# Two windowed-attention layers: the tile order of all engines, the cosine product's source and the layout of the keys

## The reference, cut to what matters

```python
h = shift_token(x)                     # second half of the channels from the token before
q, k, v = split(h @ wqkv, 3)           # 512 wide each
q = l2norm(q) * qs; k = l2norm(k) * ksc
q = q * cos * scale + rotate_half(q) * sin * scale
k = k * cos / scale + rotate_half(k) * sin / scale
# local attention: 64 queries see the 64 keys of their own window and the 64 of the window before
sim = (q * 8) @ k.T; sim = where((i < j) | (i > j + 64) | (j == -1), -max, sim)
o = softmax(sim) @ v
x = x + o @ wo
x = x + gated_gelu_mlp(layer_norm(shift_token(x)))
```

## Time and profile before

| | us |
|---|---|
| median of 3 runs | 1483.24 (1483.23 to 1484.29) |
| the profiled execution | 1488.5, of which the span from first to last instruction is 1486.8 |
| window stage of layer 0, from its first instruction to its last residual | 633.9 to 955.6 |
| window stage of layer 1 | about 1047 to 1368.8 |
| busy in the span: PE, DVE, ACT, POOL | 1283.7, 1194.9, 933.0, 743.3 |

### The profile page before, as it was taken

How to read it: one execution, slowest core, us unless ns; L and a number is a source line. 1 busy time by engine, 2 the same in 40 slices (tenths; PEclk the granted TensorE clock), 3 DMA queues, 4 the chain that set the end, 5 groups by cost and what they waited for, 6 DMA issues and landing times. The chain is left out here.

```text
span 1486.8 us, 30399 instructions
## 1 busy us (share of the span) xinstructions
PE 1283.7 (86%) x10501; PEld 712.6 (48%) x10501; DVE 1194.9 (80%) x3044; ACT 933.0 (63%) x2597; POOL 743.3 (50%) x742
## 2 busy tenths in 40 slices
PE   4579999999999997359999999699689999996992
PEld 2323333343333333326666666555356666665551
DVE  5577888888888860669999999666599999996667
ACT  4415777777677674647888888332378888884220
POOL 2001212221221221469999999210599999993102
PEclk9757999999999997679999999899899999999896
DMA  5412111112111001001211111000002111110001
GB/s 116 134 62 68 36 56 48 37 36 61 43 37 49 24 6 67 31 22 30 50 30 30 30 30 30 8 1 1 21 23 51 33 32 31 30 30 9 1 1 57
DMA packets 35056, 55.46 MB, mean 37 GB/s; under 512 B 6978, under 2 KB 22732, under 8 KB 32588
## 3 DMA queue, kind: packets, MB, share of 16 engines
q1 hardware_dynamic: 34328, 53.37, 13.5%
q10 hardware_dynamic: 576, 0.15, 0.0%
HBM read 26.77 MB, written 8.39 MB: 24 GB/s over the span
## 5 line engine op out<-in xcount | busy, mean ns | idle before, releaser
L512 ACT ACTIVATE a_prob<-a_psE 128x512 f32<-128x512 f32 (+3 forms) x768 | 318.6, 500 | 142.7 <-PE a_psE L440 140.3
L428 PE MATMUL a_psM<-a_ks,a_qs 72*128 72x512 bf16 (+3 forms) x768 | 252.3, 347 | 17.4 <-PEq L76 15.2
L595 DVE CUSTOM_DVE_ANT_0 a_psM<-a_psM,mask_q 128x384 f32<-128x384 f32 (+3 forms) x512 | 242.4, 507 | 30.7 <-PE a_psM L428 30.1
L440 PE MATMUL a_psE<-a_qs,a_ks 84*128 84x512 bf16 (+3 forms) x768 | 250.7, 339 | 16.5 <-ACT a_prob L512 8.3
L1082 POOL TENSOR_TENSOR w_t<-w_raw,w_sin 128x256 f32<-128x256 f32 x256 | 240.1, 966 | 46.9 <-ACT w_raw L1008 46.9
L547 POOL TENSOR_SCALAR_AFFINE_SELECT a_prob<-a_prob 128x512 f32<-128x512 f32 x128 | 81.1, 635 | 335.7 <-ACT a_prob L512 311.1
L597 DVE TENSOR_REDUCE a_nm<-a_psM 128x1 f32<-128x512 f32 x256 | 175.8, 687 | 47.3 <-PE a_psM L428 47.3
L1031 ACT ACTIVATE w_prob<-w_psS,w_bias 128x128 f32<-128x128 f32 x512 | 180.9, 366 | 48.8 <-DVE w_bias L1160 43.2
L1092 POOL TENSOR_TENSOR w_rn<-w_ssm,mhalf 128x16 f32<-128x16 f32 x64 | 189.4, 2959 | 0.0
L440 PEld LDWEIGHTS a_psE<-a_qs,a_ks 84*128 84x128 bf16 x768 | 75.0, 98 | 181.3 <-ACT a_prob L512 97.1
L1087 POOL TENSOR_TENSOR w_rot<-w_t 128x1024 f32<-128x1024 f32 x64 | 152.9, 2389 | 8.8 <-issue 0.4
(11 more groups left out here) (139 smaller groups left out, 2529.9 us busy)
## 6 DMA issues: line engine op xcount, KB each, us to landing
w_vb<-w_v SPq DMA_DIRECT2D x128, 128.0 KB, 2.3
a_qs<-q_parts SPq DMA_DIRECT2D x16, 576.0 KB
a_ks<-k_parts SPq DMA_DIRECT2D x16, 576.0 KB
q_parts<-p_parts SPq DMA_DIRECT2D x24, 128.0 KB
k_parts<-p_parts SPq DMA_DIRECT2D x24, 128.0 KB
out_x<-l_y SPq DMA_DIRECT2D x8, 256.0 KB, 2.3
a_qs<-a_nmT SPq DMA_DIRECT2D x32, 48.0 KB
w_wqkv<-in_wqkv SPq DMA_DIRECT2D x2, 768.0 KB, 7.2
```

The lines of the kernel that those rows point to most:

```text
L428: pe.matmul(out, qs[0:ROWS, g, j, i * P:(i + 1) * P], ks[0:ROWS, g, j, 512 * kc:512 * kc + n], start=True, stop=True).then_inc(m_ready, 1)
L440: pe.matmul(psE[:, r % NRING, 0:w], ks[0:KROWS, g, j, kt * P:(kt + 1) * P], qs[0:KROWS, g, j, q0:q0 + w], start=True, stop=True).then_inc( ...
L512: act.activation(prob[G % NPROB][:, j, 0:w], psE[:, r % NRING, 0:w], ACT.Exp, scale=SCALE0).then_inc(e_read, 1)
L595: dve.tensor_tensor_reduce(scores, scores, sb["mask_q"][:, 512 - n:512], -1.0, -3.0 * NEG, ALU.add, ALU.min, low).then_inc(m_read, 1)
```

## The change

It touches `window` alone, and the mask constant of that stage.

- **The lists.** Each slot now projects q and k of tile s+2 and v of tile s+1, turns and scores tile s-1, and weights tile s-2; tile s-3 is put out first. Slots run from -2 to NT+2. `turn_p` is cut: its first half stands ahead of `scores`, its second behind. On DVE `normalise`, `divide` and `residual` stand first.
- **POOL** does norms(t) and then rotate(t), of the same tile.
- **The cosines** are multiplied straight from psQK in PSUM instead of from raw, and t1 has two buffers. `project_qk` therefore also waits for t1_done, and `copy_raw` no longer does.
- **The keys** of a batch lie in one row, kT[P, 2, 4, 64 + 1024], and each tile is copied to its place behind the one before. The copy L1153 and its semaphore are gone; both windows' scores read 128 keys in a row from there. The order of keys changes with it, so v's copy and the mask change halves.

```diff
-        t1, t2 = tile("w_t1", [P, 2 * INNER]), tile("w_t2", [P, 2 * INNER])
+        t1, t2 = tile("w_t1", [P, 2, 2 * INNER]), tile("w_t2", [P, 2 * INNER])
-        qT, kT = tile("w_qT", [P, 2, 4, P]), tile("w_kT", [P, 2, 4, KEYS])
+        qT, kT = tile("w_qT", [P, 2, 4, P]), tile("w_kT", [P, 2, 4, WIN + S])
...
-            for s in range(NT + 4):
-                slot(s, s % 4, False)
+            for s in range(-2, NT + 3):
+                slot(s)
...
                     at_least(pe, raw_done, base, t, 0)
+                    at_least(pe, t1_done, base, t, 0)
...
+                half, first = t // TB % 2, t % TB * P
                 for c in range(4):
                     cols = slice(c * P, (c + 1) * P)
...
+                    for u in range(2):
+                        for w in range(2):
+                            rows = slice(DH * w, DH * w + DH)
+                            i = pe.matmul(psS[WIN * u:WIN * u + WIN, w, cols], qT[rows, p, c, WIN * u:WIN * u + WIN],
+                                          kT[rows, half, c, first + WIN * u:first + WIN * u + P], start=False, stop=True, skip_group_check=True)
...
-                for used in (t1_done, t2_done):
-                    at_least(act, used, base, t, -1)
+                at_least(act, t2_done, base, t, -1)
...
-                pool.tensor_tensor(rot[:, r % 2, :], t1[:, :], t2[:, :], ALU.add).then_inc(rot_done, 1)
+                pool.tensor_tensor(rot[:, r % 2, :], t1[:, r % 2, :], t2[:, :], ALU.add).then_inc(rot_done, 1)
...
-            pipelined(pool, NT, 4, [(1, norms), (0, rotate)])
+            for t in range(NT):
+                norms(t, t % 4)
+                rotate(t, t % 4)
...
-                at_least(dve, rot_done, base, t, 0)
-                dve.tensor_tensor(t1[:, :].rearrange("p (w h d) -> p w h d", w=2, d=DH), raw[:, r % 2, :].rearrange("p (w h d) -> p w h d", w=2, d=DH),
+                at_least(dve, rot_done, base, t, -1)
+                dve.tensor_tensor(t1[:, r % 2, :].rearrange("p (w h d) -> p w h d", w=2, d=DH), psQK[:, :, :].rearrange("p w (h d) -> p w h d", d=DH),
                                   cos[:, t % TB, :, :].unsqueeze(2).broadcast_to((P, 2, HEADS, DH)), ALU.mult).then_inc(t1_done, 1)
...
-                at_least(dve, prev_copied, base, t, 0)
-                dve.tensor_copy(kT[:, p, :, 0:P], psT[:, 1, :].rearrange("p (c n) -> p c n", c=4)).then_inc(kT_copied, 1)
-
-                halves(dve, s_done, t, -2)
-                dve.tensor_copy(kT[:, p, :, P:KEYS], kT[:, 1 - p, :, WIN:P]).then_inc(prev_copied, 1)
+                dve.tensor_copy(kT[:, t // TB % 2, :, WIN + t % TB * P:WIN + t % TB * P + P],
+                                psT[:, 1, :].rearrange("p (c n) -> p c n", c=4)).then_inc(kT_copied, 1)
```

More of the change, by code:

```diff
@@ L917, in scores @@
                               sb["mask_w"][:, t % TB, :].unsqueeze(1).broadcast_to((P, 4, P)), start=True, stop=False, skip_group_check=True)
+                half, first = t // TB % 2, t % TB * P
                 for c in range(4):
                     cols = slice(c * P, (c + 1) * P)
[L920 to L926, removed]
-                        i = pe.matmul(psS[WIN:P, w, cols], qT[rows, p, c, WIN:P], kT[rows, p, c, 0:P], start=False, stop=True, skip_group_check=True)
+                    for u in range(2):
[3 more added lines that the diff above has]
+                                          kT[rows, half, c, first + WIN * u:first + WIN * u + P], start=False, stop=True, skip_group_check=True)
                 i.then_inc(s_done, 2)
@@ L1177, in residual, with slot @@
                 dve.tensor_tensor(sb["xf"][:, t, :], sb["xf"][:, t, :], psO[:, 0:P], ALU.add).then_inc(xf_done, 1)
-            def slot(s, r, whole):
+            def slot(s):
                 def runs(t):
-                    return whole or 0 <= t < NT
-                r2, r3 = (r - 2) % 4, (r - 3) % 4
+                    return 0 <= t < NT
+                if runs(s - 1):
+                    normalise(s - 1, (s - 1) % 4)
                 if runs(s - 2):
-                    copy_kT(s - 2, r2)
+                    divide(s - 2, (s - 2) % 4)
                 if runs(s - 3):
-                    divide(s - 3, r3)
-                if runs(s - 4):
-                    residual(s - 4, r)
-                if runs(s):
-                    cosines(s, r)
-                if runs(s - 2):
-                    maxima(s - 2, r2, 0)
-                if runs(s + 2):
-                    carry(s + 2, (r + 2) % 4)
-                if runs(s - 3):
-                    copy_pT(s - 3, r3)
-                if runs(s - 1):
-                    normalise(s - 1, (r - 1) % 4)
-                if runs(s - 2):
-                    maxima(s - 2, r2, 1)
-                if runs(s):
-                    sums(s, r)
+                    residual(s - 3, (s - 3) % 4)
+                if runs(s - 1):
+                    copy_kT(s - 1, (s - 1) % 4)
+                if runs(s + 1):
+                    cosines(s + 1, (s + 1) % 4)
+                if runs(s - 1):
+                    maxima(s - 1, (s - 1) % 4, 0)
+                if runs(s - 2):
+                    copy_pT(s - 2, (s - 2) % 4)
+                if runs(s - 1):
+                    maxima(s - 1, (s - 1) % 4, 1)
+                if runs(s + 1):
+                    sums(s + 1, (s + 1) % 4)
+                if runs(s + 3):
+                    carry(s + 3, (s + 3) % 4)
             carry(0, 0)
-            carry(1, 1)
             slots(dve, slot)
@@ L1506, in constants @@
     c["c_sel"] = sel
[L1509 to L1510 removed]
+    ok = (i % WIN <= j) & (j <= i % WIN + WIN)
     mask = np.broadcast_to(ok[:, None, :], (P, TB, P)).copy()
[L1512 removed]
+    mask[:WIN, 0, :WIN] = False
     c["c_mask_w"] = np.where(mask, 0.0, NEG).astype(bf)
```

96 lines of the change are left out of this document (42 added, 54 removed).

## The result

The changed kernel is slower by 1.4%: 1506.19 us, median of 4 runs (1505.26 to 1507.16), where the kernel before, run beside it, took 1483.76 us (1483.23 to 1485.10, 4 runs). The ratio is 1.0141, with a 95% interval of 1.0129 to 1.0154. The forecast was 1473.0, with a range of 1453 to 1482. The profiled execution took 1506.04, its span 1504.3, at a mean granted clock of 0.931 (0.926 before).

The account below looks back on a forecast made before the run. The prediction took a closed chain of PE with DVE, 9.12 us a tile, as the bound; with fill and drain it won 5.1 us a layer, so 1478.3 profiled, less 5.26 to the median: 1473.0 us, range 1453 to 1482.

Parts of the forecast that it names:

- PE's chain: Closed chain of PE with DVE, once a tile in mid stage: claimed to set the period at 9.12 us (9.06 to 9.18).
- Now four transposes stand there, about 0.45: On PE, between the transposes of q and k and the scores: about 0.45 us of work standing there.
- The last term: End of PE's chain: DVE's copy of the keys, 0.69 us, and 0.06 to PE, where the next mask begins.
- the last slots: Drain of a layer, last three slots: 8.5, 8.25 and 11.2 us, set at 28.0 together.
- The fill: Start of a layer: bounded by POOL, with the scores of tile 2 starting at 676.0 us.
- POOL's turn without the lock: POOL's work a tile once the sine products are not held up: 8.19 us, 0.97 less.
- The signs named ahead: Signs in the profile: period 9.06 to 9.18 us, two PE waits a tile, POOL idle about 1 us a tile.
- A loop of DVE: Rival: DVE's loop, with its wait for the scores, sets the period at about 8.8 us, 1456 in all; chance 0.14.
- The lock was avoided: Rival denied here: cosines from PSUM still block POOL's sine products, period 9.2 to 9.25 us, 1478 in all; chance 0.10.
- The product from PSUM: Rival: the cosines' product from PSUM is slow; at twice 1.22 us it adds 0.5 a tile, 1500; chance 0.05.
- The power didn't hold up DVE: Rival denied here: normalise and divide wait 2.95 us for POOL's power, 1592 us in all; chance 0.01.
- PE's clock: Rival: a lower clock lengthens PE's chain, by 0.27 us a tile at 0.95 granted, 1487 in all; chance 0.08.

Follow-up runs that it names:

- early_q: The changed kernel, with ACT's copy of q waiting for its own four transposes, not all eight: 1478.45 us, ratio to before 0.9943.
- cos_raw: The changed kernel, with the cosines multiplied from the copy in SBUF (raw) again, not from PSUM: 1504.22 us, one run.
- out_between: The changed kernel, with `out` moved between the transposes of q and k and the first half of `turn_p`, `residual` behind the cosines: 1467.26 us, ratio to before 0.9879.
- p0_behind: The changed kernel, with the first half of `turn_p` moved behind the scores, next to the second: 1531.08 us, one run.
- v_between: The changed kernel, with `project_v` moved between the transposes of q and k and the first half of `turn_p`: 1487.36 us, ratio to before 1.0017.
- mask_q_raw: The changed kernel, with the mask ahead of `turn_p`'s first half, q copied after its own four transposes, cosines from SBUF: 1481.55 us, one run.
- b_keys: The kernel before, with only the keys of a batch in one row and no copy L1153: 1537.42 us, ratio to before 1.0337.

## Why the prediction was wrong

**The step that failed** is in PE's chain: "Now four transposes stand there, about 0.45", counted as cover for the copies. They can't cover ACT's copy, since they wait for it. That `turn_p` waits for the copies of q and k stood in the description of the kernel before. The prediction set ACT aside by its busy time and asked only whether its copy ends before DVE's. It does (808.00 against 808.09), but the four transposes come between it and the mask. The last term, 0.75 for the copy of k and the way to PE, should have been 0.60 + 0.14 + 0.47 = 1.21. With the other terms as measured that makes 9.50 in place of 9.12 (the first copy took 0.61 where 0.66 was set). early_q shows that this wait is in what sets the period: one copy starts 0.43 earlier, and the period is 0.41 shorter.

**In the sum**, 27 steps at 0.38 are 10.3 us a layer, 20.5 for both. The last residual of layer 0 came at 961.78, not 950.2: 10.3 of it from the steps, the rest from the last slots (27 steps behind the mask of tile 2 came 932.2, and 29.6 us more, where 28.0 were set). Layer 1's end is another 16.2 late: its own steps (10.4 with the unrounded period), 4.5 in its last slots, which took 32.5 us, and some 1.2 on the way to its tile 2, whose mask came at 1096.94. The last four residuals of layer 1 took 34.6 us where layer 0's took 31.7, in a stretch (1350 to 1386) with a granted clock of 0.91, against 1.00 in layer 0's (930 to 962). That the clock did this was not tested by an edit, but cos_raw points the same way: these four steps took 35.5 us in its layer 0 at 0.86 and 33.2 in its layer 1 at 0.95. So the profiled execution missed its forecast of 1478.3 by 27.7. The other 5.4 are the step from the profiled execution to the median. The one of before was 5.26 above its median, and I took that off; after's is 0.15 below its own. One execution's distance to the median was no property of the kernel.

**What was right.** The fill: the mask of tile 2 was at 675.53, set at 676.0. POOL's turn without the lock, 8.19 us set, 2.91 + 2.77 + 0.13 + 2.35 = 8.16 measured. Normalise beside the power at 1.23, the cosines from PSUM at 1.22 (the row had pointed to 1.22). PE's part from `values` to the transposes, 4.19 set and 4.18 measured. The bound was PE's chain and not POOL's or DVE's list, though the chain runs through ACT's copy as well.

**The signs named ahead** said it at once: "the period is under 9.0 or over 9.25" was its own test for being wrong. It also expected PE to wait twice, for k ahead of the mask and for the probabilities ahead of the second half of values; the first wait was of 0.78 and for q, the second hardly there (0.4 us in 25 tiles).

**The rivals.** None was this one. A loop of DVE came to bind in out_between, at 8.87, but it is not the predicted one, and that the two sums agree is chance: it leaves DVE at `normalise` and goes through the transposes, `out` and the first half of `turn_p` to the scores, where the predicted one went from the copy of the keys straight to the mask. The lock was avoided. The product from PSUM was not slow. The power didn't hold up DVE. PE's clock was 1.00 in mid stage; the lower clock went with about 3 us more at the end of layer 1. The rival on the slow side that was missing is the plain one: a wait of the moved instruction itself. The ring through ACT was missing too. In the order of the change it is nearly as long as the chain: mask to exponentials 2.42 and those 2.75 in the trace of after, 0.69 to `out` and 1.00 for it as in v_between, 1.81 to `turn_p` and 0.47 to the mask, 9.14. I learned of it only from p0_behind and v_between.

**The part of the change that pays** is that POOL's 9.16 falls to 8.2. It took two edits, neither on POOL or DVE, to cash it in, the mask's place on PE and an earlier signal from PE to ACT: 9.50 to 8.64.

## What to carry to other kernels

Before work is counted as cover for a wait, look at what that work waits for itself: here the transposes into a shared PSUM tile wait for the copy that reads it. When a bound is removed, write down every ring through the engines with its sum, those through the engine that is "busy less" too; here the order decided which of four rings was the longest, at 8.64 to 9.99 us, and a matmul group put into the gap of one ring lengthened another. And where two engines hold each other up, as POOL and DVE do here, removing an instruction moves all that follow it: the time must be worked out again for which product meets which.

## What the runs showed of the hardware

- In these runs a DVE product with both operands in SBUF doesn't wait for POOL's power, also when it starts 0.14 us behind it (mask_q_raw: power at 806.72, normalise at 806.86 for 1.22 us, the power 2.90). But a power whose turn comes while such a product still runs takes longer by about what the product still needs (b_keys: 3.90 for 2.91, the division ending 1.13 us behind the power's start). So the two seem to get in each other's way only at the power's start; that is read from these two cases, and no run tested it by itself.
- The Trainium skill (SBUF — State Buffer, SBUF: two separate sides) has whichever of the two starts first hold the pair of ports for the whole instruction. For the division that started on POOL's sum the trace of b_keys agrees: it took 2.79 us for 1.23. For a product that starts behind the power it doesn't: 1.22 in mask_q_raw. The measurement decides.
- A product that reads one operand from PSUM beside POOL's sine products cost neither engine anything in the changed kernel (1.22 and 2.77); from SBUF, in cos_raw and mask_q_raw, the four sine products take 3.76 to 3.78 and the cosines up to 1.47.
